# A vision tower's first attention: q and k turned by products of column halves, an earlier rotation, and the causal mask added by TensorE

## What is computed

```python
qkv = x @ W_attn + b_attn
q, k, v = jnp.split(qkv, 3, axis=-1)
...
q = q * cos + _rotate_half(q) * sin
k = k * cos + _rotate_half(k) * sin
att = jnp.einsum('bhqd,bhkd->bhqk', q, k) * D ** (-0.5)
causal = jnp.tril(jnp.ones((T, T), dtype=bool))
att = jnp.where(causal, att, -jnp.inf)
att = jax.nn.softmax(att, axis=-1)
y = jnp.einsum('bhqk,bhkd->bhqd', att, v)
```

## Time and profile before

| | |
|---|---|
| median of 3 runs | 773.21 us (765.08, 773.21, 773.70) |
| profiled execution | 780.8 us, span 779.1 us |
| TensorE busy (matmul) | 719.9 us, 92% |
| VectorE busy | 499.6 us, 64% |
| ScalarE busy | 368.2 us, 47% |
| GpSimd busy | 166.2 us, 21% |
| mean granted TensorE clock | 0.915 |

### The profile page before, as it was taken

How to read it: one execution, slowest core, us unless ns; L and a number is a source line. 1 busy time by engine, 2 the same in 40 slices (tenths; PEclk the granted TensorE clock), 3 DMA queues, 4 the chain that set the end, 5 groups by cost and what they waited for, 6 DMA issues and landing times.

```text
span 779.1 us, 15686 instructions
## 1 busy us (share of the span) xinstructions
PE 719.9 (92%) x6062; PEld 636.3 (82%) x6062; DVE 499.6 (64%) x1239; ACT 368.2 (47%) x850; POOL 166.2 (21%) x166
## 2 busy tenths in 40 slices
PE   7699999999998889899899999899999989889996
PEld 6478888999997566678796788789999976779996
DVE  1537657888868862646745385367767667746785
ACT  0158645455544213457623342245554547547662
POOL 2200004544433202224302000006443420000000
PEclk9855599999999978889979999799999999899999
DMA  9900201223212000000200010011322200102100
GB/s 269 285 0 2 76 2 55 75 75 126 86 57 62 1 1 0 3 1 2 91 4 0 1 42 2 2 57 42 96 72 72 70 21 2 50 4 79 63 21 23
DMA packets 16199, 38.79 MB, mean 50 GB/s; under 512 B 3577, under 2 KB 4569, under 8 KB 15740
## 3 DMA queue, kind: packets, MB, share of 16 engines
q1 hardware_dynamic: 14150, 36.71, 15.6%
q10 hardware_dynamic: 1976, 1.08, 0.6%
HBM read 37.32 MB, written 0.44 MB: 48 GB/s over the span
## 4 chain that ended last, share of the span: by engine, by line
PE 67%; DVE 20%; ACT 4%; issue 4%; POOL 3%; DMA 1%; POOLq 0%; ACTq 0%; DVEq 0%; SPq 0%
PE PS L703 8%; PE PS L757 5%; PE PS L659 4%; PE PS L543 4%; PE PS L547 4%; PE PS L545 4%; PE PS L546 4%; PE PS L544 4%; PE PS L692 3%; PE PS L595 3%; PE PS L722 2%; POOL ssq L1772 2%; DVE AL L1416 2%; PE PS L597 2%; PE PS L599 2%
## 5 line engine op out<-in xcount | busy, mean ns | idle before, releaser
L926 ACT ACTIVATE MIX<-PS 128x288 f32<-128x288 f32 x118 | 48.5, 412 | 114.7 <-PE PS L547 114.4
L543 PE MATMUL PS<-XH,WH 128*128 128x288 f32 x284 | 86.7, 305 | 3.6 <-DVE OT L1405 1.4
L1745 POOL TENSOR_TENSOR rstd<-var,nhalf 96x3 f32<-96x3 f32 x18 | 15.3, 851 | 322.9 <-DVE var L1202 322.9
L545 PE MATMUL PS<-XH,WL 128*128 128x288 f32 x284 | 84.0, 296 | 0.0
L544 PE MATMUL PS<-XL,WH 128*128 128x288 f32 x284 | 84.0, 296 | 0.0
L546 PE MATMUL PS<-X,WH 128*128 128x288 f32 x284 | 84.0, 296 | 0.0
L547 PE MATMUL PS<-X,WL 128*128 128x288 f32 x284 | 83.9, 295 | 0.0
L1405 DVE TENSOR_TENSOR OT<-MIX,PS 128x288 f32<-128x288 f32 x94 | 42.2, 450 | 39.7 <-ACT MIX L926 39.0
L1416 DVE TENSOR_TENSOR AL<-OT,AH 128x288 fp32r<-128x288 f32 x118 | 58.9, 508 | 3.3 <-ACT AH L940 2.3
L1259 DVE TENSOR_TENSOR WL<-RG,WH 128x768 fp32r<-128x768 f32 (+2 forms) x46 | 57.7, 1257 | 3.5 <-ACT WH L906 3.3
L595 PE MATMUL PS<-AH,DW 128*128 128x288 f32 x166 | 52.7, 318 | 7.2 <-DVE AL L1416 7.0
(11 more groups left out here) (233 smaller groups left out, 1745.8 us busy)
## 6 DMA issues: line engine op xcount, KB each, us to landing
RG<-in_gu_l0f_dram SPq DMA_DIRECT2D x8, 512.0 KB, 4.2
RG<-in_gu_l0f_dram SPq DMA_DIRECT2D x16, 256.0 KB, 5.4
RG<-in_gu_l2f_dram SPq DMA_DIRECT2D x9, 384.0 KB, 3.5
RG<-in_gu_l2f_dram SPq DMA_DIRECT2D x18, 192.0 KB, 4.2
RD<-in_wd_l0f_dram SPq DMA_DIRECT2D x8, 384.0 KB, 3.0
RD<-in_wd_l2f_dram SPq DMA_DIRECT2D x9, 288.0 KB, 2.8
RD<-in_wd_l3f_dram SPq DMA_DIRECT2D x6, 384.0 KB, 3.5
BIG<-in_patch_dram SPq DMA_DIRECT2D x6, 288.0 KB, 6.9
```

Of the source, the lines that this page charges most:

```text
L543: mm(o, WH[r][:, 0, w], XH[:, cols], start=True, stop=False)
L545: mm(o, WL[r][:, 0, w], XH[:, cols], start=False, stop=False)
```

## The change

1. Turning q and k in A0: TX holds q and k once, 64 columns apart, with 48 used. Instead of 6 transposes of 112 by 96, TensorE runs 12 products with 64 weight columns each and 48 moving columns of the identity, one for the even and one for the odd images, into partitions 0 to 63 and 64 to 127. The rest of the 64 weight columns is zero.
2. The queries of both halves are then written by one operation over 112 partitions: three activations on ScalarE in A0 instead of six. In A3 the q product is 64 wide, VectorE's three operations cover 112 partitions, and ScalarE's three with `q1_sb` go.
3. The causal mask of A0 is added by TensorE: a product of the identity with the mask (108 by 108, 288 columns, the mask repeated for each image) opens each unit's group of scores, and the scores accumulate on it. VectorE's mask addition goes; it takes maximum and difference from PSUM.
4. The rotation of unit 0 (with the four small scaled weights) moves on VectorE from the start of `attention` to right behind the layer norm of the second half, before the copies of the turned half.
5. QB is no longer cleared, and less of TX.

```diff
                         pe.wait_ge(S["q_sb"], U)
                         pe.wait_ge(S["k_sb"], U)
-                        if a.paired and not a.tm:
-                            pe.wait_ge(S["q1_sb"], u)
                     for k in range(2):
-                        if a.paired and not a.tm:
+                        if a.paired and a.tm:
+                            for tau in range(TAU):
+                                for r in range(2):
+                                    o = (2 * tau + k) * VW
+                                    last = mm(PS[VW * r:VW * (r + 1), k, tau * TP // 2:(tau + 1) * TP // 2].rearrange("f (i m) -> f i m", m=NB),
+                                              TX[u % 2][:, o:o + VW],
+                                              cst[0:TP, 0:TP].rearrange("p (i r m) -> p r i m", r=2, m=NB)[:, r],
+                                              start=True, stop=True)
+                        elif a.paired:
+                            wide = VW if k == 0 else a.fq
                             for r in range(2):
                                 for c in range(NC_):
                                     off = (2 * g + k) * a.fq
-                                    last = mm(PS[VW * r:VW * r + a.fq, k, 0:HN // 2].rearrange("f (b n) -> f b n", n=N),
-                                              W[0:CB[c], c, off:off + a.fq], xv_half(c, j, CB[c])[:, r:HB:2, :],
+                                    last = mm(PS[VW * r:VW * r + wide, k, 0:HN // 2].rearrange("f (b n) -> f b n", n=N),
+                                              W[0:CB[c], c, off:off + wide], xv_half(c, j, CB[c])[:, r:HB:2, :],
                                               start=(c == 0), stop=(c == NC_ - 1))
                         elif a.tm:
...
                     U = u0 + u
                     pe.wait_ge(S["q_sb"], U + 1)
                     pe.wait_ge(S["k_sb"], U + 1)
-                    if a.paired and not a.tm:
-                        pe.wait_ge(S["q1_sb"], u + 1)
                     if u == 0:
                         pe.wait_ge(S["v_sb"], V0[a.name] + a.vpieces)
                     if u >= 1:
                         pe.wait_ge(S["s_taken"], U)
+                    masked = a is A0
+                    if masked:
+                        mm(PS[0:a.rows, 5, 0:HN], cst[0:a.rows, 0:a.rows],
+                           masks[:, 0, :].unsqueeze(1).to_broadcast([a.rows, HB, N]), start=True, stop=False, skip_group_check=True)
                     for i in range(HB // 2 if a.paired else 0):
                         last = mm(PS[0:a.rows, 5, 2 * i * N:2 * (i + 1) * N], QB[u % 2][0:VW + a.fq, i, 0:a.rows],
-                                  KS[u % 2][0:VW + a.fq, 2 * i * N:2 * (i + 1) * N], start=True, stop=True)
+                                  KS[u % 2][0:VW + a.fq, 2 * i * N:2 * (i + 1) * N], start=not masked, stop=True, skip_group_check=masked)
...
                         i = PS[0:a.fq, 1, 0:HN].rearrange("f (t p) -> f t p", t=TAU)
                     else:
                         o, i = KS[u % 2][0:a.fq, :], PS[0:a.fq, 1, 0:HN]
-                    if a.paired and a.tm:
+                    if a.paired:
+
                         if u == 0:
-                            act.wait_ge(S["qk_pads"], 1)
-                        for r in range(2):
-                            last = activation(by_turned(KS[u % 2][VW * r:VW * r + a.fq, :], r), pair_view(1, r), ACT.Copy)
-                        last.then_inc(S["k_sb"], 1)
-                    elif a.paired:
-
-                        if u == 0:
-                            act.wait_ge(S["qk_pads"], 2)
+                            act.wait_ge(S["qk_pads"], PADDED.index(a) // 2 + 1)
                         for r in range(2):
                             rows = slice(VW * r, VW * r + a.fq)
+                            if a.tm:
+                                o = KS[u % 2][rows, :].rearrange("f (i r m t) -> f r t i m", r=2, m=NB, t=TAU)[:, r]
+                                last = activation(o, PS[rows, 1, 0:HN // 2].rearrange("f (t i m) -> f t i m", t=TAU, m=NB), ACT.Copy)
+                                continue
                             last = activation(KS[u % 2][rows, :].rearrange("f (i r n) -> f i r n", r=2, n=N)[:, :, r],
                                               PS[rows, 1, 0:HN // 2].rearrange("f (i n) -> f i n", n=N), ACT.Copy)
                         last.then_inc(S["k_sb"], 1)
-
-                        for h in range(a.hg):
-                            last = activation(QB[u % 2][rows, 0:HB // 2, h * N:(h + 1) * N],
-                                              PS[rows, 0, 0:HN // 2].rearrange("f (i n) -> f i n", n=N), ACT.Copy,
-                                              scale=mh[rows, h:h + 1])
-                        last.then_inc(S["q1_sb"], 1)
                     elif a.qk_norm:
                         activation(o, i, ACT.Identity, bias=qn[:, 3:4], scale=qn[:, 2:3]).then_inc(S["k_sb"], 1)
...
@@ -1057,11 +1051,11 @@
                         if a.qk_norm:
                             o, i = q_views(a, u, h)
                             last = activation(o, i, ACT.Identity, bias=qs[:, 2 * h + 1:2 * h + 2], scale=qs[:, 2 * h:2 * h + 1])
-                            continue
-                        for r in range(2):
-                            rows = slice(VW * r, VW * r + a.fq)
-                            o = QB[u % 2][rows, 0:HB // 2, h * N:(h + 1) * N].rearrange("f i (m t) -> f t i m", t=TAU)
-                            last = activation(o, pair_view(0, r), ACT.Copy, scale=mh[rows, h:h + 1])
+                        else:
+                            rows = VW + a.fq
+                            o = QB[u % 2][0:rows, 0:HB // 2, h * N:(h + 1) * N].rearrange("f i (m t) -> f t i m", t=TAU)
+                            last = activation(o, PS[0:rows, 0, 0:HN // 2].rearrange("f (t i m) -> f t i m", t=TAU, m=NB), ACT.Copy,
+                                              scale=mh[0:rows, h:h + 1])
...
@@ -1133,10 +1127,9 @@
 
             def clear_pairs():
 
-                zero = nhalf[:, 0:1].to_broadcast([128, 4 * 128])
+                zero = nhalf[:, 0:1].to_broadcast([128, HN])
                 for r in range(2):
-                    activation(QB[r][:, 0:HB // 2, :].rearrange("p i n -> p (i n)"), zero, ACT.Copy, scale=0.0)
-                    last = activation(KS[r][:, :], zero[:, 0:HN], ACT.Copy, scale=0.0)
+                    last = activation(KS[r][:, :], zero, ACT.Copy, scale=0.0)
                 last.then_inc(S["qk_pads"], 1)
 
...
                     normalised(n, src, j).then_inc(S["ln_normed"], 1)
 
+            def rotate(a, u):
+
+                u0, f2 = UNIT0[a.name], TAU * 2 * a.fq
+                src, t2 = PSF[0:TP, 1024:1024 + f2], T2[:, 0:f2]
+                if u == 0:
+                    dve.wait_ge(S["qk_pads"], 1)
+                if u >= 2:
+                    dve.wait_ge(S["qk_ready"], u0 + u - 1)
+                dve.wait_ge(S["tm_ready"], TM0[a.name] + u + 1)
+                co = rope[:, 0, :, :].rearrange("p t f -> p (t f)")
+                si = rope[:, 1, :, :].rearrange("p t f -> p (t f)")
+                V.tensor_tensor(T2[:, f2:2 * f2], src, co, ALU.mult)
+                V.tensor_tensor(t2[:, 0:f2:2], src[:, 1:f2:2], si[:, 0:f2:2], ALU.mult)
+                link(V.tensor_tensor(t2[:, 1:f2:2], src[:, 0:f2:2], si[:, 1:f2:2], ALU.mult))
+                V.tensor_tensor(TX[u % 2][:, 0:2 * TAU * VW].rearrange("p (n x) -> p n x", x=VW)[:, :, 0:a.fq],
+                                T2[:, f2:2 * f2].rearrange("p (n x) -> p n x", x=a.fq),
+                                t2.rearrange("p (n x) -> p n x", x=a.fq), ALU.add).then_inc(S["tm_done"], 1)
+
+            def first_rotation(a):
+
+                dve.wait_ge(S["in_const"], 16 * (len(consts) - FIRST))
+                for h in range(2):
+                    V.tensor_scalar(qs[:, 2 * h:2 * h + 1], qn[:, 0:1], mh[:, 3 + h:4 + h], None, ALU.mult)
+                    last = V.tensor_scalar(qs[:, 2 * h + 1:2 * h + 2], qn[:, 1:2], mh[:, 3 + h:4 + h], None, ALU.mult)
+                link(last)
+                rotate(a, 0)
+
             def second_half_in(k):
 
                 kind, a = STAGES[k]
                 if kind != "moe":
                     evac_xt(k, kind, a, 0)
                 layer_norm(k, 1)
+                if a is A0:
+                    first_rotation(a)
                 if kind != "moe":
...
@@ -1572,15 +1575,14 @@
                 def queries(u):
                     U = u0 + u
                     dve.wait_ge(S["qk_ready"], U + 1)
-                    if u == 0 and a.paired:
-                        dve.wait_ge(S["qk_pads"], 2)
                     if U >= 2:
                         dve.wait_ge(S["s_ready"], U - 1)
+                    rows = VW + a.fq
                     for h in range(a.hg if a.paired else 0):
 
-                        last = V.tensor_scalar(QB[u % 2][0:a.fq, 0:HB // 2, h * N:(h + 1) * N],
```

(60 more changed lines are left out.)

4 lines of the change are left out of this document (removed).

## The result

| | before | after |
|---|---|---|
| median | 773.7 us (765.08 to 781.36, 13 runs) | 762.9 us (759.88 to 768.48, 13 runs) |
| ratio | | 0.989 (95% interval 0.985 to 0.9925) |
| profiled execution | 780.8 us, span 779.1 | 763.16 us, span 761.4 |
| mean granted clock | 0.915 | 0.946 |

The account below looks back on a forecast made before the run. TensorE was taken to bound the first attention, nearly all at half clock; at full clock its steps, outputs and tail end at 91.4 instead of 107.4 us, with the last attention minus 16.4, forecast 761.5 us, range 751 to 769.

Parts of the forecast that it names:

- VectorE's crowded units: First attention, where weight splits crowd two units of VectorE: 1.0 us allowed in all at full clock.
- tail: From the output products to the addition to H in the first attention: 9.1 us, at full clock already.
- the main case: First attention: with the hole closed the clock stays up, the stage ends at 91.4 instead of 107.4 us; chance 0.50.
- half clock throughout: Rival: clock stays at half through the first attention, added work counts double, 778 us, or 784 with serial turning; chance 0.22.
- a fall when the values end: Rival: the clock holds at first, then falls at about 56 us in the first attention; gain 4.4, 769 us; chance 0.14.
- The third, no difference: Rival: the median runs of before had the clock up already in the first attention; 3 us gained, 770; chance 0.14.
- the hole of 1.85 us: TensorE's wait for VectorE's first rotation at 36 to 38 us; closing it saves 1.85 us and keeps the clock up.
- ScalarE drops off the path: First attention: three QB activations instead of six save 1.36 us a unit; of ScalarE's 5.7 us a unit 4.4 remain.
- its 0.75 us a unit: VectorE in the first attention: smaller TX and no mask addition save this, worth nothing while TensorE needs more a unit.
- The second of its two guesses: On the median 7.6 us below the profiled execution: its runs may keep the first attention's clock already, leaving less to gain.
- The last attention: QB written whole by VectorE, three activations and one wait go: minus 0.4 us (0 to 1.0).
- The floor for short products: Turning q and k: by the skill's rule 48 columns would cost a quarter more, 2.4 us instead of 1.96 at half clock.

Follow-up runs that it names:

- before again: The kernel before, unchanged, profiled once more for a second look: 773.88 us, one run.
- fillers: Products of 384 columns that nobody reads, two in each of loop steps 5 to 8, added to the changed kernel with six query activations: 772.83 us, ratio 0.999.
- the hole filled: The kernel before with three added products of 384 columns that nobody reads, ahead of the second token-major product where TensorE sat idle: 771.63 us, ratio 0.997.

## Why the prediction was right or wrong

**The number**: 761.5 was predicted, 762.9 measured. Of the sum nearly every term of the first attention held.

| term | predicted | measured |
|---|---|---|
| loop, from unit 1's token-major product | 40.7 | 40.04 |
| turning q and k | 0.9 | 0.84 |
| mask and scores | 0.50 + 0.91 | 0.67 + 0.73 |
| token-major product | 1.5 | 1.54 to 1.76 |
| probabilities, mix | 0.56, 0.65 | 0.37, 0.56 |
| 24 output instructions | 4.4 | 4.12 |
| VectorE's crowded units | 1.0 | 0.2, inside the 40.04 |
| tail | 9.1 | 9.09 |
| H in the chain | 91.4 | 88.18 |

H came 3.2 us before the forecast: 1.3 because the loop began at 34.93 instead of 36.2 (the whole program runs about 1 us earlier in this execution), 0.7 in the loop, 0.3 in the outputs, and the 1.0 allowed for VectorE. Two sums of the text are a little off and carry nothing: the parts named for a unit without values make 5.8 us and not 6.0 (the chain has 5.7 to 6.0), and 8 x 0.4 + 7 x 0.4 around 761.5 is 755.5 to 767.5, not 751 to 769.

**The clock** was the step on which most depended, and the main case was right: 1.00 from 36 us to the outputs. The first two rivals are out for this kernel: half clock throughout, and a fall when the values end. The third, no difference, is out by its time of 770, but its premise, that the median runs of before had the clock up already, was right for about half of the stage.

**The reason given for it was wrong in its weight.** The text put the hole of 1.85 us as what decides the stage. Without the early rotation the changed kernel loses 3 us; with it alone before gains 7.5 and loses the clock at 57 us. That "TensorE has work without a break" once the hole is closed came true only with the halved ScalarE work.

**The step that failed** is "ScalarE drops off the path", priced at nothing. Its own condition, "if this cover were gone, it would be back as in the earlier trace rows", hid the error: at half clock ScalarE's 5.7 us lay just under TensorE's 6.0, but at full clock, where the forecast put the kernel, TensorE needs 4.9, and six activations stand out. The wait of 0.77 us in the earlier trace rows was only the end of it: the chain of before runs through ScalarE for 8.4 us in one piece, from here to the scores at 88.42.

```profile
79.98 0.36 ACT KS L1027
...
87.92 0.46 ACT QB L1064
```

That a halved ScalarE goes with the clock staying up was not seen, though the earlier trace rows showed a wait and the rival "clock no difference" named the 5.7. Measured by giving them back: 10.1 us of the medians, 9.8 in the stage. The same holds for VectorE: its 0.75 us a unit were worth nothing by the text; the mask's part alone measured 5.0 of the medians, 2.9 in the stage.

**The parts don't add.** Taken out of the changed kernel one at a time they cost 3.1, 5.0 and 10.1 us, together more than its 10.8: as far as these runs show, each is needed for one thing, that TensorE has no gap. Added one at a time to before, the rotation gives 7.5 and the mask product takes 3.2. The halved ScalarE work alone was not run on before, and the turning by column halves, the smaller TX and the last attention's part were never undone by themselves.

**The median.** The text left open why the profiled execution lay 7.6 us above it. The second of its two guesses holds: the run of before at the median has the clock back at full from about 43 to 66 us, so 12.1 us were there to gain in the stage and not 19.2. That the forecast landed so near is in part luck, by this hedge: taken whole, the first attention's gain of 16.0 from the median would have given 757.

**The last attention** should have given 0.4 us. From the values group to H it takes 40.7 us, where before again has 39.3 (633.09 to 672.43): the loop is 0.1 shorter, but the outputs fall at half clock for longer, 7.43 us against 6.01. VectorE held that loop, busy for 9.66 of the last 10 us ahead of the fall in both. The gap just before the fall was longer (TensorE busy for 0.67 of 2 us, where before again has 0.92); whether that made the clock stay down longer isn't shown. The forecast looked for what its queue waits for, not for the clock behind it. Behind that attention's last H (668.0 us) the changed kernel took 93.4 us where before again took 90.7; since the run with the mask on VectorE took 90.6 there, this belongs to the execution and not clearly to the change.

**The floor for short products.** The rule cited in the text, of the Trainium skill's page "TensorEngine Tiling (Array Packing)", section "Instruction Overhead", would have made the turning dearer. The 24 instructions took 35 ns each (0.84 us in the chain after), less than 48 columns one behind another at the 0.86 ns of the earlier trace rows, so the two column halves do overlap; whether a floor lies under that, these rows don't say.

## What to carry to other kernels

Read each engine's load per unit at the clock that the change is meant to bring, not at the one that the profile shows: an engine hidden at half clock is the bound at full. Where TensorE is nearly always busy, ask of each engine that feeds it whether it leaves a gap of a us or two, since the gap costs its own length and can cost a stretch at half clock behind it. Work may even be moved onto TensorE for that, but only where the engine that it leaves was the one that opened the gap; where TensorE is the bound it costs its own length, and fillers do too. And compare stages between profiles, not whole times: away from the stage under study, two executions here differed by up to 9 us (665.6 to 674.4 behind H).

## What the runs showed of the hardware

- The clock fell from 1.00 to 0.50 shortly behind stretches of 2 us with TensorE busy for 0.15, 0.57, 0.76, 0.78 and 1.26. But in before again a stretch with 0.96 at 58 us was followed by 6 us more at 1.00, and with the hole filled the same stretch, 0.96 at 58 us too, was followed by the fall near 62. A gap stands ahead of all falls seen in this stage; not every gap brings one, and what else decides is open.
- The rise is as uneven. In the profiled execution of before the clock stayed at 0.50 over 42 us of work without a break; in before again the same instructions had it back within a few us, and without the early rotation the changed kernel had it back 3 us after the fall. No run here says why.
- Two instructions of 288 columns that open the group took 0.67 us in the chain and the eight scores behind them 0.73, where scores alone had taken 0.91: the sum was as predicted, the split was not.
- One operation of VectorE on 96 x 288 elements from SBUF to SBUF, the last of the first rotation, took 1.65 us at 32.32 in the changed kernel, while GpSimd added the bias to H (31.03 to 33.65), and 0.46 in the run with the rotation late, behind that addition. It cost nothing here, since TensorE did not wait; that GpSimd is the cause is likely and was not tested.
